# Four chained layers on one core: attention splits moved from GpSimd to VectorE and ScalarE, and the output projection dealt out over 22 of 32 units

## The reference

```
x = x + einsum('bct,bcd->bdt', x, W0[cond])                  # L0: one of 16 32x32 matrices per sample
x = x + x(d) @ base_weight.T + bias + lora_B[id] lora_A[id]   # L1: base product and an adapter per sample
x = x + attention(x)                                          # L2: see below
x = x + einsum('bct,bcd->bdt', x, W3[cond])                  # L3
```

```
k_all = concat([k_cache[block_table], k]); v_all = concat([v_cache[block_table], v])
scores = einsum('bqhd,bkhd->bhqk', q, k_all) * SCALE, masked
o = softmax(scores) @ v_all
out = einsum('bse,de->bsd', o, Wo)          # Wo: 512 x 4096
```

## Time and profile before

| | |
|---|---|
| median of 3 runs | 2390.94 us (2390.47 to 2391.7) |
| the profiled execution | 2394.14 us, its span 2392.4 us |
| PE busy | 2312.0 us, 97% of the span |
| PE weight loads | 2010.2 us, 84% |
| DVE busy | 1760.8 us, 74% |
| ACT busy | 1535.2 us, 64% |
| POOL busy | 1395.5 us, 58% |
| DMA | 455.96 MB, mean 191 GB/s |

### The profile page before, as it was taken

How to read it: one execution, slowest core, us unless ns; L and a number is a source line. 1 busy time by engine, 2 the same in 40 slices (tenths; PEclk the granted TensorE clock), 3 DMA queues, 4 the chain that set the end, 5 groups by cost and what they waited for, 6 DMA issues and landing times.

```text
span 2392.4 us, 58277 instructions
## 1 busy us (share of the span) xinstructions
PE 2312.0 (97%) x15392; PEld 2010.2 (84%) x15392; DVE 1760.8 (74%) x5422; ACT 1535.2 (64%) x4221; POOL 1395.5 (58%) x2249
## 2 busy tenths in 40 slices
PE   8999999999998899999999999999999999998999
PEld 5778888888887788888888888888888888887777
DVE  4434777777778887887887887887887887886232
ACT  4324666666667777777777777777777777775221
POOL 1003454444447777877877877877877877872000
PEclk9999999999998999999999999999999999999999
DMA  4335333333337777777767777777767777775332
GB/s 164 95 110 163 102 98 102 111 106 102 97 115 257 221 224 239 253 228 237 255 223 241 253 228 237 255 223 242 252 220 245 253 223 241 253 221 194 110 132 101
DMA packets 347959, 455.96 MB, mean 191 GB/s; under 512 B 34506, under 2 KB 280842, under 8 KB 343695
## 3 DMA queue, kind: packets, MB, share of 16 engines
q1 hardware_dynamic: 308398, 315.83, 41.9%
q0 software_dynamic: 36864, 134.23, 16.9%
q10 hardware_dynamic: 2528, 4.29, 0.5%
HBM read 374.53 MB, written 79.69 MB: 190 GB/s over the span
## 4 chain that ended last, share of the span: by engine, by line
PE 48%; DVE 23%; issue 19%; ACT 5%; POOL 3%; DMA 1%; DVEq 0%; ACTq 0%; POOLq 0%; SPq 0%
PE S L1168 11%; PE oP L1168 11%; DVE regC L987 8%; PE S L1260 7%; DVE k_lo L284 7%; PE oP L1241 3%; PE oP L1092 3%; DVE regC L986 3%; PE S L1209 3%; PE bank L1092 2%; PE oP L1122 2%; ACT regC L721 2%; PE bank L1260 2%; DVE nmx L975 1%; DVE rinv L981 1%
## 5 line engine op out<-in xcount | busy, mean ns | idle before, releaser
L1241 PE MATMUL oP<-regC,regK 128*128 128x128 f32 x4096 | 541.2, 275 | 0.1
L1241 PEld LDWEIGHTS oP<-regC,regK 128*128 128x128 f32 x4096 | 507.2, 192 | 9.6 <-issue 0.3
L975 DVE CUSTOM_DVE_ANT_0 regC<-S,mask 128x544 f32<-128x544 f32 x512 | 368.1, 719 | 187.9 <-issue 185.7
L715 ACT CAST k_hi<-regK 128x544 fp32r<-128x544 f32 x512 | 331.3, 647 | 210.5 <-PE S L1209 184.1
L721 ACT ACTIVATE regC<-regC,nmx 128x544 f32<-128x544 f32 x512 | 384.9, 752 | 58.8 <-DVE nmx L975 49.8
L534 POOL TENSOR_TENSOR regC<-regC 128x256 f32<-128x256 f32 x320 | 244.3, 784 | 278.3 <-DVE regC L944 278.3
L549 POOL TENSOR_TENSOR q_hi<-regC,ones 128x128 fp32r<-128x128 f32 x512 | 262.3, 512 | 233.8 <-PE S L1209 229.1
L1092 PE MATMUL bank<-ident,regC 128*128 128x128 f32 x2048 | 321.1, 279 | 26.9 <-ACT regC L765 21.0
L284 POOL TENSOR_TENSOR k_lo<-regK,k_hi 128x192 fp32r<-128x192 f32 x512 | 341.4, 667 | 3.3 <-ACT k_hi L715 3.3
L987 DVE TENSOR_SCALAR regC<-regC,rinv 128x512 f32<-128x512 f32 x512 | 337.8, 660 | 0.0
L284 DVE TENSOR_TENSOR k_lo<-regK,k_hi 128x352 fp32r<-128x352 f32 x512 | 328.2, 641 | 2.9 <-ACT k_hi L715 2.9
(11 more groups left out here) (137 smaller groups left out, 4468.9 us busy)
## 6 DMA issues: line engine op xcount, KB each, us to landing
regK<-kT_cache SPq DMA_DIRECT2D x1024, 128.0 KB
qkT_d<-regC SPq DMA_DIRECT2D x160, 256.0 KB, 2.3
regC<-qkT_d SPq DMA_DIRECT2D x64, 512.0 KB
oT_d<-regC SPq DMA_DIRECT2D x64, 256.0 KB
regK<-oT_d SPq DMA_DIRECT2D x16, 1024.0 KB, 5.0
regC<-wqk SPq DMA_DIRECT2D x10, 1024.0 KB, 5.2
v_d<-regC SPq DMA_DIRECT2D x32, 256.0 KB, 2.3
regK<-qkT_d SPq DMA_DIRECT2D x64, 128.0 KB
```

The lines of the kernel that those rows point to most:

```text
L715: nc.scalar.copy(k_hi[u % 2].rearrange("p (s t) -> p s t", t=PSIZE), k_sb[b][:, :, h, :]).then_inc(s_khi, 1)
L975: nc.vector.tensor_tensor_reduce(out=p_sb[u % 4], in0=scores, in1=mask[u // HK % 2][:], scale=-SCALE, scalar=3e38, op0=ALU.add, op1=ALU.mi ...
L1241: last = nc.tensor.matmul(oP[:, j * 512:j * 512 + P], v_sb[b][:, m, u % HK * D:(u % HK + 1) * D], pT_sb[u % 2][:, m * P:(m + 1) * P], star ...
```

## The change

- POOL makes no splits any more; only its index copies and gathers stay. Since nothing paces it in these steps, it runs on to its next wait (s_po).
- q_hi is made by ACT and q_lo by DVE, four units at once (512 columns), in two buffers.
- k_lo is made whole by DVE (544 columns), one unit later in its order: split_k(u+3), at the head of the step.
- DVE's step is now split_k(u+3), masked_max(u+2), inverse(u+1), normalise(u+1), then mask, split_q and out_low where due. The mask has one buffer, not two.
- ACT's step is own copy, exps(u+1), split_k(u+4), pT copy, heads, q_hi.
- PE's turn_p always follows the score, and turn_own ends the step u % 4 == 3.
- The 48 matmuls of the output projection are dealt out one by one: two to a step, three in the steps 1, 5, 9 and 13, over 22 steps: 30, 31 and 0 to 19 of the next group. So that the heads of the next group have room meanwhile, oT_hi and oT_lo have six slots; in every other group the first two samples lie in slots 4 and 5, and the projection reads slots 2 to 5. The rows of x2r follow that order, so it is loaded and stored in two pieces. The residual moves to step 21.
- The loops go over two groups at a time. Q has a semaphore of its own; SP loads Q first, then waits for s_klo and loads own K and pages. The block table is loaded group by group. w3 is loaded after the attention.

```
-WO_AT = {UG - 2: 0, UG - 1: 2, 0: 4, 1: 6, 2: 8, 3: 11, 4: 14, 5: H2}
-LOW = 11
+SLOTS = 6
+WO_AT = {u: 3 if u in (1, 5, 9, 13) else 2 for u in (UG - 2, UG - 1, *range(20))}
+WO_END = 21
...
+        def slot_of(o, par, b):
+            k = 4 + b if par and b < 2 else b
+            return o.rearrange("p (j r n) -> p j r n", j=4, n=SLOTS * C)[:, :, :, k * C:(k + 1) * C]
...  SP
-                        sp.wait_ge(s_qp, g * UG + HK * (k + 1))
-                        load_own(b, k % 2)
+                        sp.wait_ge(s_qp, g * (2 * BT) + 2 * (k + 1))
+                        load_q(b, k % 2)
                         sp.wait_ge(s_klo, g * UG + HK * (k + 1))
-                        load_pages(b, k % 2)
+                        load_own_k(b, k % 2)
+                        load_pages(btab[0:1, par, k * NPP:(k + 1) * NPP], k % 2)
...  POOL
-                if not (fixed and n + 4 >= NU):
-                    split_q(n + 4, u + 4, g * 2 + (u + 4) // (2 * HK))
...  ACT, step
+                if not (fixed and n + 1 >= NU):
+                    exps(n + 1, u + 1)
                 if not (fixed and n + 4 >= NU):
                     split_k(n + 4, u + 4, g * 2 + (u + 4) // (2 * HK))
-                if u % 4 == 0:
-                    if not (fixed and n + 2 >= NU):
-                        exps(n + 2, u + 2)
-                    if not (fixed and n == 0):
-                        out_heads(g, u)
                 act.wait_ge(s_ta, n + 1)
                 ge(act, s_pv, n - 1)
                 nc.scalar.copy(pT_sb[u % 2], pT).then_inc(s_evA, 1)
-                if u % 4 and not (fixed and n + 2 >= NU):
-                    exps(n + 2, u + 2)
+                if u % 4 == 0 and not (fixed and n == 0):
+                    out_heads(g, u, par)
+                if u % 4 == 2 and not (fixed and n + 6 >= NU):
+                    split_q(g * (UG // 4) + (u // 4 + 2), u + 6, g * 2 + (u + 6) // (2 * HK))
...  DVE, step
-                if not (fixed and n + 1 >= NU):
-                    inverse(n + 1, u + 1)
+                if not (fixed and n + 3 >= NU):
+                    split_k(n + 3, u + 3)
                 if not (fixed and n + 2 >= NU):
                     masked_max(n + 2, u + 2, g * BT + (u + 2) // HK)
                 if not (fixed and n + 1 >= NU):
+                    inverse(n + 1, u + 1)
                     normalise(n + 1, u + 1)
-                if not (fixed and n + 4 >= NU):
-                    split_k(n + 4, u + 4)
+                if u % HK == 5 and not (fixed and n + 3 >= NU):
+                    make_mask(g * BT + (u // HK + 1))
+                if u % 4 == 3 and not (fixed and n + 5 >= NU):
+                    split_q(g * (UG // 4) + (u // 4 + 2), u + 5)
                 if u % HK == 4:
-                    out_low(g, u // HK)
-                if before is not None and u == 6:
+                    out_low(g, u // HK, par)
+                if before is not None and u == WO_END:
                     residual(before)
...  PE, step
-                if u % 4 == 0 and not (fixed and n == 0):
-                    turn_own(g, u)
                 if not (fixed and n + 2 >= NU):
-                    score(n + 2, u + 2)
-                if u % 4:
-                    turn_p(g, u)
+                    score(n + 2, u + 2, g * (UG // 4) + (u + 2) // 4)
+                turn_p(g, u)
                 of = g if u >= UG - 2 else before
-                if u in WO_AT and WO_AT[u] < H2 and of is not None:
-                    out_proj(of, WO_AT[u], WO_AT[(u + 1) % UG])
+                if u in WO_AT and of is not None:
+                    out_proj(of, par if of is g else 1 - par, WO_FROM[u], WO_AT[u])
                 if u > 0:
                     values(g, u - 1)
...
-                if u % 4 == 0:
-                    turn_p(g, u)
+                if u % 4 == 3:
+                    turn_own(g, u)
```

More of the change, by code:

```diff
@@ L174, in build @@
         q_sb = [inC(HK * P) for _ in range(2)]
-        oT_hi = parts("oT_hi", H2 * P)
-        q_hi, q_lo = [parts("q_hi0", P)], [parts("q_lo0", P)]
-        k_hi, k_lo = zip(*([parts(f"{name}{i}", KW) for name in ("k_hi", "k_lo")] for i in range(2)))
+        w3_sb = q_sb[0][:, 0:CONDS * C].rearrange("p (k d) -> p k d", k=CONDS)
         o_st = inC(T)
         x2r = inC(T)
+        pT_sb = [inC(L) for _ in range(2)]
+        q_hi, q_lo = [parts("q_hi0", HW)], [parts("q_lo0", HW)]
+        k_hi = [parts("k_hi0", KW)]
         po_sb = [inC(P) for _ in range(2)]
+        pTo_sb = inC(P)
+        assert at[0] <= 12 * T
+        at[0] = 12 * T
+        k_lo = [None, parts("k_lo1", KW)]
+        k_hi.append(parts("k_hi1", KW))
+        q_hi.append(parts("q_hi1", HW))
+        q_lo.append(parts("q_lo1", HW))
         p_next = [inC(KW) for _ in range(3)]
[L183 to L186, removed]
+        oT_hi, oT_lo = (parts(f"oT_{part}", SLOTS * H2 * C) for part in ("hi", "lo"))
+        assert at[0] >= 27 * T
         p_sb = [inC(KW)] + p_next
-        q_hi.append(parts("q_hi1", P))
-        q_lo.append(parts("q_lo1", P))
-        o3_hi, o3_lo = ((y, x) for x, y in zip((oT_hi, oT_lo), o3_parts))
+        k_lo[0] = parts("k_lo0", KW)
+        assert at[0] == CSZ
+        o3_hi, o3_lo = ((y, x[:, 0:H2 * P]) for x, y in zip((oT_hi, oT_lo), o3_parts))
         xy = [o_st, x2r]
-        ones = sb("ones", [P, P])
-        mask = [sb(f"mask{i}", [P, KW]) for i in range(2)]
+        mask = sb("mask", [P, KW])
         ident = sb("ident", [P, P])
@@ L259, in build @@
         s_k = [sem(f"s_k{i}") for i in range(2)]
+        s_q = [sem(f"s_q{i}") for i in range(2)]
         s_v = [sem(f"s_v{i}") for i in range(2)]
@@ L407, in _, with rows_of, load_rows, store_rows @@
             sp.dma_start(wo_raw, wo[0]).then_inc(s_wo_in, 16)
-            def group(g, first, last):
+            def rows_of(g, par):
+                for i in range(2):
+                    a = (1 - i if par else i) * 2 * C
+                    yield x2r[i * 2 * C:(i + 1) * 2 * C, :], x2_d[bass.ds(g, 1), a:a + 2 * C].rearrange("a p n -> p (a n)")
+            def load_rows(g, par):
+                for here, there in rows_of(g, par):
+                    sp.dma_start(here, there).then_inc(s_x2r, 16)
+            def store_rows(g, par):
+                for here, there in rows_of(g, par):
+                    sp.dma_start(there, here).then_inc(s_x2yst, 16)
+            def group(g, par, first, last):
                 for k in range(BT):
@@ L916, in _ @@
                 split_w(VB, 0, c)
-            for i in range(2):
-                nc.vector.memset(mask[i][:, L:KW], 0.0)
+            nc.vector.memset(mask[:, L:KW], 0.0)
             nc.vector.tensor_copy(seqf[:], seqi)
@@ L1198, in block_qk, with score @@
                     if last and t == NT - LAG:
-                        score(0, 0)
-            def score(n, u):
+                        score(0, 0, 0)
+            def score(n, u, m):
                 pe.wait_ge(s_klo, n + 1)
-                pe.wait_ge(s_qp, n + 1)
+                if u % 4 == 0:
+                    pe.wait_ge(s_qp, m + 1)
                 ge(pe, s_mx, n)
+                head = slice(u % 4 * P, (u % 4 + 1) * P)
                 halves = (slice(0, 9 * PSIZE), slice(9 * PSIZE, KW))
-                for m, (q, k) in enumerate(((q_hi, k_hi), (q_hi, k_lo), (q_lo, k_hi))):
+                for i, (q, k) in enumerate(((q_hi, k_hi), (q_hi, k_lo), (q_lo, k_hi))):
                     for at in halves:
-                        last = nc.tensor.matmul(scores[:, at], q[u % 2], k[u % 2][:, at],
-                                                start=(m == 0), stop=(m == 2))
+                        last = nc.tensor.matmul(scores[:, at], q[u // 4 % 2][:, head], k[u % 2][:, at],
+                                                start=(i == 0), stop=(i == 2))
                 last.then_inc(s_qk, 1)
```

224 lines of the change are left out of this document (122 added, 102 removed).

## The result

The changed kernel takes 2399.67 us (median of 20 runs, 2387.84 to 2406.82) against 2390.64 (20 runs, 2388.73 to 2393.16): ratio 1.0034, 95% interval 1.0025 to 1.0042. It is slower by 0.34%; 2336 was forecast, with a range up to 2372. The profiled execution has a span of 2391.8 us and is one of the quicker of the 20.

What follows compares the result with a forecast made beforehand. PE was taken to bound the attention, losing 6.9 of 90.0 us a group. Saving 3.6 in 15 groups (54.0), plus 1.5, minus 0.5, took 55.0 off 2394.1; the median, 3.2 lower, gave 2336, range 2302 to 2372.

Steps and rivals of the forecast that it cites:

- the sentence on the loops: Attention loops over two groups: the halved jumps back were valued at zero, at most 0.8 us.
- that of POOL: POOL's V gathers, no longer metered by its splits, would go out all four at once (2.1 MB) into the K pages.
- rival (3): SP's queue: gather burst delays K pages, at least 4.6 us a group, 2405 us or more; chance 0.10.
- The pages themselves hide as before: SP's K pages: 20.7 us from gate to use in the bare block, 14.7 to the last issue.
- The group: One attention group of 32 units would take 86.4 us instead of 90.0, saving 3.6.
- DVE's 0.43 us a unit back: DVE's scalings and k_lo would shorten by 0.43 us a unit once POOL's arithmetic is gone.
- bare units 2.1: Score starts of plain attention units without projection matmuls would be 2.1 to 2.2 us apart.
- The stall behind the out heads: DVE's oT_lo and k_lo delay PE's scores: 0.8 us after steps 20 and 28, 0.1 in the other two blocks.
- The first group: The attention's first group, with other work (the splits of Wo on ACT and DVE), was given a saving of 1.5 us.
- Rivals (1): PE reaches its floor because slack covers DVE's stalls: 83.9 us a group, 2298 us; chance 0.13.
- (2): DVE is dearer, 2.30 us a unit: 88.7 us a group, 2370 us; chance 0.22.
- (4): PE is already full at 97% and nothing follows from the change: 2391 us; chance 0.05.

Runs made afterwards that it cites:

- f1: The changed kernel with all attention loops unrolled and its V gathers spread one a unit by waits on POOL: 2340.29 us, ratio 0.9787.
- f2: The changed kernel, loops kept, with only POOL's V gathers spread over four units by a wait: 2382.52 us, ratio 0.9968.
- g3: f2 with the loops of PE, ACT and DVE unrolled and SP's kept: 2347.52 us, ratio 0.9815.
- e1: The changed kernel with the attention loops of all five engines unrolled, gathers still in a burst: 2395.26 us, ratio 1.0020.
- e2: The kernel before with only the attention loops of PE, ACT, DVE and SP lengthened to two groups: 2411.9 us, ratio 1.0090.
- h2: e1 with each gather fetching a quarter of each row for 62 of 64 samples, same issues: 2390.05 us, ratio 1.0003.
- e4: The changed kernel's division of labour and order, with the old projection in seven steps, four slots and one-group loops: 2538.12 us, ratio 1.0607.
- g1: e1 with the four gathers of a sample still in one burst, but three units later: 2431.76 us, ratio 1.0169.
- f3: e4 with the gathers spread over four units by a wait on POOL: 2398.9 us, ratio 1.0035.
- f4: f1 with DVE's K split done one step sooner, ahead of the low half of the out heads: 2322.35 us, ratio 0.9711.
- h1: e1 with the four gathers of a sample issued in two separate pairs: 2341.7 us, ratio 0.9799.
- e3: The changed kernel with SP's attention loop alone unrolled, gathers in a burst: 2456.47 us, ratio 1.0287.
- g2: f2 with SP's attention loop alone unrolled: 2383.52 us, ratio 0.9971.

## Why the prediction was wrong

From after to f1 the steps are, from 2399.7: the burst 17.2 (to f2), the jumps of PE, ACT and DVE 35.0 (to g3), the loops of SP and POOL with the small operation that carries the wait in f2 and g3, 7.2 (to f1): 2340.3. (By the ratios to the kernel before, each measured beside it: 16, 37 and 7.) The steps add up by construction, and their sizes depend on the order: with the burst left in, unrolling gives 4.4 (e1), and spreading the gathers then 55. But the trace of after, without the other runs, divides its own loss in the same way: 35.5 us in the groups with a jump and 18.1 in the others. f1 is the kernel as the forecast saw it, jumps and gathers free, within 4.3 us of the 2336 given for it.

**The step that failed first** is the sentence on the loops: "No row shows a stall of PE that only a jump explains: zero, and 8 x 0.1 = 0.8 at most." It took the price of a jump from a body of one group and carried it to one of two. Shown by g3 against f2: 35.0 us; by e2, in the other kernel: 21.5; and by PE's branch itself, 3.5 to 4.7 us against 0.21. The page gives a hint at the mechanism: the two instruction queues carry 118 and 217 packets after,

```profile
q8 instruction: 118, 1.93, 0.3%
q14 instruction: 217, 1.78, 0.2%
```

against 28 and 141 before. Straight code, in which every group is loaded once, has 108 and 160 (e1): the loops over two groups load more than no loops at all, so the code is loaded again at each turn, and the loops over one group load far less. Counted in the trace from one jump to the next, with the waits and register instructions that it lists, a turn is 286 instructions on DVE, 238 on ACT and 1522 on PE before, and 599, 500 and 3040 after. The Trainium skill (Runtime: NRT & Kernel Launch, Instruction fetch mechanics) has an engine hold 512 instructions, PE 2048, and a taken branch out of what is held stop it until the target is fetched. One group fits by that rule, and two don't on DVE and PE, and the trace agrees with it there. ACT's 500 would fit by the figure, and it stops all the same, for 2.7 to 3.2 us; the measurement decides, so the figure is not to be taken as the exact point. Worked out at the time the rule would have been a rival. No run has a body in between.

**The second** is that of POOL: "POOL no longer meters the gathers by its splits: all four (2.1 MB) go out at once behind s_po, into the pages." It was seen, priced in rival (3) and given 0.10. In the changed kernel it acted as that rival has it, pages late, 20.3 us of waits, 17.2 us of time; the forecast's "The pages themselves hide as before" is what f2 shows without the burst. Its argument against the rival, that both kinds of load had overlapped before, passed over their spacing: 2.7 us and more between gathers then, 1.24 now. The measured 2399.67 lies near that rival's 2405, which is luck: the rival had nothing of the jumps, the larger part of the loss. But the price was worked out of bytes at 239 GB/s, and h2 shows that bytes are not what it depends on, e4 that the pages need not be there. Semaphore updates that come 1.7 us late (g1) are the larger form of it: the late starts counted above make 54 us in e1, which lost 55, and 94 in e4, which lost 139 and whose clock is also at half for 61 us of the attention (none in f3). Why the looped kernel after is spared that form, with the same burst, stays open; so does the hardware's reason. The half clock behind a stop of PE, which no sum of the forecast has, is a part of both costs.

**What held.** The group: 86.4 forecast, 86.8 in f1, 87.1 in after's good ones. DVE's 0.43 us a unit back; k_lo near 0.71; bare units 2.1; no row of PE released by POOL. The stall behind the out heads was forecast at 2 x 0.8 + 2 x 0.1 = 1.8 us a group; f4, which takes it away, is 1.0 faster a group (86.82 to 85.78) and 17.9 in all. The first group was under-sized: 98.8 to 91.6 in f1, 7.2 gained where 1.5 was given, and the other groups gained 3.1 to 3.2 against 3.6 (two of them only 1.9). The two errors have opposite signs, and that f1 comes within 4.3 us of 2336 owes something to it. Rivals (1), (2) and (4) are out by the units themselves.

## What to carry to other kernels

When work is taken off an engine, ask what that work was metering: here POOL's splits spaced its gathers, and with them went a pacing that nobody had written down; one wait brought it back and was worth 17 to 139 us. Price a jump by the length of its own body, not by that of a shorter one. When the good groups of a trace agree with the forecast and the bad ones alternate, look for what happens every second time.

## What the runs showed of the hardware

Four indirect DMAs of 128 rows issued 1.3 us apart can hold up the semaphores of several engines: a matmul's waiters start 1.7 us late (g1) and 2.4 (e4), and at a quarter of the bytes the loss is nearly the same (h2). In the changed kernel the same burst shows none of it, for a reason that stays open. Two together cost nothing that shows (h1, 2341.7 against 2340.3). Unrolling SP alone cost 57 us with the burst (e3 against after), where such late starts make 57, and 1 us without it (g2 against f2). A jump back over two groups holds PE's sequencer for 3.5 to 4.7 us, over one group for 0.21, and in the changed kernel the granted clock is at half for 3.4 or 6.8 us behind each of its six.
